# A DLRM tower on one core: the Gram matrices in 128x32 column tiles

## The chip, the cores and the metric

The kernel runs on one NeuronCore of a Trainium2 chip. The metric is the device time of one execution in microseconds (us), the median of three runs. Engines are named as in the profile: PE is TensorE's matmul side and PEld its weight loads, DVE is VectorE, ACT is ScalarE, POOL is GpSimd, SP is SyncE. TensorE's clock has two levels here, 2.4 GHz (a granted clock of 1.0) and 1.2 GHz (0.5).

## The reference, cut to what matters

```python
e = jnp.stack([tbl_0[ids[:, 0]], ..., tbl_26[ids[:, 26]]], axis=1)   # (2048, 27, 128)
dot = jnp.einsum('bnd,bmd->bnm', e, e)                                # one 27x27 Gram per sample
z = dot.reshape(2048, 27 * 27)[:, idx]      # the 351 pairs i < j
h = jnp.concatenate([z, dense_ctx], axis=1)                           # (2048, 367)
h = jnp.maximum(h @ W_top1 + b_top1, 0.0)                             # (2048, 512)
h = jnp.maximum(h @ W_top2 + b_top2, 0.0)                             # (2048, 256)
y = h @ W_top3                                                        # (2048, 1)
```

Everything is float32. Each of 2048 samples takes 27 rows of 128 numbers from 27 tables. Its Gram matrix holds all the dot products of these rows.

## The kernel before, in words

The samples are worked through in 8 bodies (`PAIRS`) of 256 samples, each of 2 tiles (`TILES`) of 128 samples. The first and the last body are written out, and the six between are passes of one loop on every engine (`sweep`). The program is written by hand: each engine has its own list of instructions, and semaphores order them.

Rows come in two ways. For 8 small tables TensorE picks them with one-hot matrices (`lookup`, line 622, four jobs of two tables in a body; VectorE builds the one-hots at line 486). For the other 19 tables GpSimd gathers rows with indirect DMAs (line 331, 38 in a body), and TensorE transposes them (`transpose_rows`, line 639, five jobs per tile). A gather of the next body may start when the transposes of this body have read its rows. In the last body four of the looked-up tables are gathered too (line 338). VectorE and ScalarE take turns to copy both into `embT` (lines 492, 496, 365 and 369), which holds 32 slots of one float for each sample, 27 of them used.

The Gram step (`gram`, line 649) multiplies four samples at once: the stationary operand has the 123 columns of four samples (three slots of 32 and 27 more), the moving one 4 x 26 columns. Only the four diagonal blocks of the product are used. A step has 8 such matmuls, that is 32 samples, and a tile has 4 steps. The steps of a tile use the two tiles `gram_ps[0]` and `gram_ps[1]` in turn. VectorE copies the blocks of the even steps to `blocks` (line 503) and ScalarE those of the odd steps (line 395), with four copies per step, one for each diagonal block (`block_views`). A step may write its bank when the copies of the step two before are done:

```python
past(pe, (gram_dve, gram_act)[s % 2], p * (TILES * STEPS // 2) + step // 2)
```

The transposes use the banks of `gram_ps` too, so that those of the second tile wait for the last copies of the first. When all steps of a tile are copied, VectorE turns the blocks (`turn`, lines 512 to 527) into `z`, and TensorE transposes `z` (line 659) for the three layers (lines 675, 683 and 690; in the last body 707 to 720). These are done one body later, between lookups and transposes. On TensorE a body is in this order:

1. `lookup` 0, transposes of z of the second tile of the body before (`layers` step 0), `lookup` 1, first layer, `lookup` 2 and 3
2. transposes of tile 0, second layer, the four gram steps of tile 0
3. transposes of tile 1, third layer, the four gram steps of tile 1
4. transposes of z of tile 0

In the first body VectorE also builds the first four one-hots of the next body between its block copies: one after each of steps 0 and 2 of each tile. In the other bodies it builds one after step 0 of each tile.

Of the kernel before, what the change touches and what calls it, by code (L numbers as in the profile page):

```python
# [28 lines left out]
ACT = mybir.ActivationFunctionType  # L29

P = 128
B, NF, D, CTX = 2048, 27, 128, 16
# [46 lines left out]
ACT_JOBS = EVERY.all - DVE_JOBS  # L79
NJ = NF - 1  # L80
Q, G = 4, 32
GS = 8
STEPS = G // GS
SHIFTS, RUN = NF // 2, 9
PAIRS_CH = SHIFTS * RUN
# [2 lines left out]
K1 = [PAIRS_CH + n for n in CTX_CH]  # L88
JEXT = NF + SHIFTS
SLOT = 32  # L90
GM = (Q - 1) * SLOT + NF
MLP_JOBS = 6
BANKS = 2
N1, N2 = H1 // P, H2 // P
# [17 lines left out]
def dlrm_tower(nc, ids, ids_mm, ident_in, dense_ctx, tables, W1, b1, W2, b2, W3, out):  # L112
    with ExitStack() as ctx:
        def sb(name, shape, dt):
            return ctx.enter_context(nc.sbuf_tensor(name, shape, dt))

        def ps(name, shape):
            return ctx.enter_context(nc.psum_tensor(name, shape, F32))

        def sem(name):  # L120
            return ctx.enter_context(nc.semaphore(name))

        def sb_view(tile, first, dims, start=0, count=P):
            full = tile[:]
            pitch = full.ap[0][0]
            return bass.AP(full.tensor, start * pitch + first, [[pitch, count], *dims])
# [18 lines left out]
        embT = sb("embT", [P, TILES, P, SLOT], F32)  # L145
        blocks = sb("blocks", [P, TILES, NJ, G], F32)
# [11 lines left out]
        gram_ps = [ps(f"gram_ps{k}", [P, 2, 512]) for k in range(2)]  # L158
# [29 lines left out]
        gram_dve = sem("gram_dve")  # L188
        gram_act = sem("gram_act")
# [7 lines left out]
        def past(eng, s, value):  # L197

            if not (isinstance(value, int) and value <= 0):
                eng.wait_ge(s, value)  # L200
# [28 lines left out]
            return (sb_view(embT, t * P * SLOT + slot, [[1, n], [SLOT, P]]),  # L229
                    emb_bank(jobs, jobs.look + t * jobs.tr + k)[:, 0:n * P].rearrange("d (f b) -> d f b", f=n))  # L230

        def block_views(t, s, q):

            src = gram_ps[s % 2][q * 32:q * 32 + NF, :, 0:4 * Q * NJ].rearrange("i h (g c) -> i h g c", g=4)
            return (sb_view(blocks, t * NJ * G + GS * s, [[4, 2], [1, 4], [G, NJ]], q * 32, NF),
                    src[:, :, :, q * NJ:(q + 1) * NJ])

        block = ctx.enter_context(nc.Block())

# [105 lines left out]
        def _(act):  # L345
# [43 lines left out]
            def keep_blocks(p, t, s):  # L389

                step = t * STEPS + s
                act.wait_ge(gram_filled, p * TILES * STEPS + step + 1)
                past(act, s_turned, (p - 1) * TILES + t + 1)
                for q in range(Q):
                    last = nc.scalar.activation(*block_views(t, s, q), ACT.Copy)  # L395
                last.then_inc(gram_act, 1)

            def last_layers(kind, t):

# [62 lines left out]
        def _(dve):  # L462
# [7 lines left out]
            def convert_ids(p):  # L470
                dve.wait_ge(s_idsb, (p + 1) * 16)

                past(dve, s_onehot, p * NM - len(ACT_ONEHOTS))
                if isinstance(p, int) and p == 1:
                    dve.wait_ge(onehot_act, len(ACT_ONEHOTS))
                nc.vector.tensor_copy(ids_f[:], ids_b[:]).then_inc(s_ids, 1)  # L476
                dve.wait_ge(s_ids, p + 1)

            def make_onehot(p, k):

                if k >= OH:
                    dve.wait_ge(emb_filled, p * EVERY.all + (k - OH) // LOOK_TABLES + 1)
                else:
                    past(dve, emb_filled, (p - 1) * EVERY.all + (k + NM - OH) // LOOK_TABLES + 1)
                for c in range(CH):
                    last = nc.vector.tensor_scalar(onehot[:, k % OH, c, :], ids_f[:, k, :], row_of[:, c:c + 1], None,  # L486
                                                   ALU.is_equal)
                last.then_inc(s_onehot, 1)

            def move_lookup(p, k):  # L490
                dve.wait_ge(emb_filled, p * EVERY.all + k + 1)
                nc.vector.tensor_copy(*lookup_views(k)).then_inc(emb_dve, 1)

            def move_rows(p, jobs, t, k):
                dve.wait_ge(emb_filled, p * EVERY.all + jobs.look + t * jobs.tr + k + 1)
                nc.vector.tensor_copy(*row_views(jobs, t, k)).then_inc(emb_dve, 1)  # L496

            def keep_blocks(p, t, s):

                step = t * STEPS + s  # L500
                dve.wait_ge(gram_filled, p * TILES * STEPS + step + 1)
                for q in range(Q):
                    last = nc.vector.tensor_copy(*block_views(t, s, q))  # L503
                last.then_inc(gram_dve, 1)

            def turn(p, t):

# [48 lines left out]
            def body(p, first, last):  # L556


                jobs = FINAL if last else EVERY
                for k in range(EVERY.look):  # L560
                    if k < jobs.look and jobs.by_dve[k] and not first:
                        move_lookup(p, k)
                    if last:
                        continue
                    if not first and (k + 1) * LOOK_TABLES <= NM - OH:
                        for f in range(k * LOOK_TABLES, (k + 1) * LOOK_TABLES):
                            make_onehot(p, OH + f)
                    if k == 1:
                        convert_ids(p + 1)
                    if k == 2 and not first:  # L570
                        make_onehot(p + 1, 0)
                        make_onehot(p + 1, 1)
                for t in range(TILES):
                    for k in range(jobs.tr):
                        if jobs.by_dve[jobs.look + t * jobs.tr + k]:
                            move_rows(p, jobs, t, k)
                    if t:
                        turn(p, 0)
                    for s in range(0, STEPS, 2):
                        keep_blocks(p, t, s)  # L580
                        if first:
                            make_onehot(p + 1, (t * STEPS + s) // 2)
                        elif not last and s == 0:
                            make_onehot(p + 1, 2 + t)
                turn(p, 1)

            sweep(dve, body)

        @block.tensor
        def _(pe):  # L590
# [51 lines left out]
            def gram(p, t, s):  # L642

                step = t * STEPS + s

                past(pe, (gram_dve, gram_act)[s % 2], p * (TILES * STEPS // 2) + step // 2)
                for g in range(GS):
                    four = embT[:, t, (GS * s + g) * Q:(GS * s + g + 1) * Q, :]
                    last = nc.tensor.matmul(gram_ps[s % 2][0:GM, g // 4, (g % 4) * Q * NJ:(g % 4 + 1) * Q * NJ],  # L649
                                            four.rearrange("d q f -> d (q f)")[:, 0:GM], four[:, :, 0:NJ],  # L650
                                            start=True, stop=True)
                last.then_inc(gram_filled, 1)

            def transpose_z(p, t):
# [125 lines left out]
```

## Time and profile before

| | |
|---|---|
| median of 3 runs | 455.84 us (454.64 to 455.99) |
| the profiled execution | 455.73 us |
| its span, first to last instruction | 453.9 us |
| mean granted TensorE clock | 0.944 |
| TensorE matmuls, weight loads | 372.9 us, 345.7 us busy, 2740 instructions each |
| VectorE, ScalarE, GpSimd | 305.8 us, 183.3 us, 303.8 us busy |
| gram matmuls (line 649) | 1024, 124.6 us busy |
| block copies, ScalarE and VectorE (lines 395, 503) | 128 and 128, 67.8 us and 65.9 us busy |

The span is taken from one profiled execution, and the 1.8 us around it are part of its time. Busy time of TensorE counts each matmul to its modelled end, so that matmuls which follow each other closely overlap in it.

### The profile page before, as it was taken

Reading aid. Unit: us, or ns where it says so; the run is one execution under the profiler, and the core shown is the slowest. Engines: PE = TensorE matmul, PEld = TensorE weight load, DVE = VectorE, ACT = ScalarE, POOL = GpSimd, SP = SyncE. Lnnn points to the kernel's source line nnn. Section 1 sums busy time; section 2 is a strip of 40 time slices with the busy share of each in tenths; the row PEclk is TensorE's granted clock in tenths of the full one; section 3 lists DMA queues with packets and bytes.
Section 4 is the critical chain, followed back from the end, with each engine's and each line's share of the span. In section 5 each row is a group of like instructions: output and inputs, shape, how many; then the busy total and the mean of one; then the engine's idle time right before and its main releaser. Section 6 shows DMA issues by size and latency. Waiting matters only on the chain.

```text
span 453.9 us, 8416 instructions
## 1 busy us (share of the span) xinstructions
PE 372.9 (82%) x2740; PEld 345.7 (76%) x2740; DVE 305.8 (67%) x719; ACT 183.3 (40%) x304; POOL 303.8 (67%) x317
## 2 busy tenths in 40 slices
PE   0652555799998999899988998999989998998577
PEld 0642555698987899689978996989878996997376
DVE  3565505989768886888688968797688867435250
ACT  1117630542444334632455146424443345435152
POOL 5777605777677767777777777777777776777300
PEclk9966865999999999999999999999999999999599
DMA  4645693422125921293225421441269221222100
GB/s 110 179 162 179 173 81 59 131 53 58 38 54 70 133 49 47 60 92 99 53 51 83 111 56 48 79 122 46 53 63 120 69 53 46 55 52 54 29 1 0
DMA packets 28189, 34.85 MB, mean 77 GB/s; under 512 B 12975, under 2 KB 21815, under 8 KB 28174
## 3 DMA queue, kind: packets, MB, share of 16 engines
q1 hardware_dynamic: 18190, 14.19, 20.4%
q0 software_dynamic: 9984, 20.47, 16.7%
q8 instruction: 8, 0.13, 0.1%
q14 instruction: 7, 0.06, 0.0%
HBM read 34.63 MB, written 0.01 MB: 76 GB/s over the span
## 4 chain that ended last, share of the span: by engine, by line
PE 54%; DVE 13%; DMA 12%; ACT 8%; issue 7%; SPq 5%; POOL 1%; POOLq 0%; ACTq 0%; DVEq 0%
PE gram_ps L649 19%; PE emb_ps L622 16%; PE mlp_ps L675 8%; DVE blocks L503 6%; DMA blocks<-in_tbl 6%; PE mlp_ps L683 5%; ACT blocks L395 5%; DMA ids_b<-in_ids_mm 3%; PE gram_ps L639 3%; ACT embT L369 3%; SPq L276 2%; DMA rows<-in_tbl,idx 2%; DVE turned L512 2%; DVE onehot L486 1%; DVE z L527 1%
## 5 line engine op out<-in xcount | busy, mean ns | idle before, releaser
L331 POOL DMA_INDIRECT rows<-in_tbl,idx x304 | 295.9, 973 | 117.5 <-DMA rows<-in_tbl,idx 86.9
L622 PE MATMUL emb_ps<-onehot,parts 125*128 125x256 f32 x960 | 130.2, 297 | 33.9 <-ACT parts L349 20.6
L622 PEld LDWEIGHTS emb_ps<-onehot,parts 125*128 125x128 f32 x960 | 124.6, 202 | 35.8 <-ACT parts L349 21.4
L486 DVE TENSOR_SCALAR onehot<-ids_f,row_of 128x256 fp32r<-128x256 f32 x464 | 143.9, 383 | 9.2 <-PE emb_ps L622 8.6
L649 PE MATMUL gram_ps<-embT 128*123 128x104 f32 x1024 | 124.6, 281 | 23.5 <-DVE embT L496 11.4
L649 PEld LDWEIGHTS gram_ps<-embT 128*123 128x123 f32 x1024 | 119.6, 195 | 31.8 <-DVE embT L496 12.7
L395 ACT ACTIVATE blocks<-gram_ps 27x208 f32<-27x208 f32 x128 | 67.8, 530 | 99.2 <-PE gram_ps L649 98.0
L503 DVE COPY blocks<-gram_ps 27x208 f32<-27x208 f32 x128 | 65.9, 515 | 46.9 <-PE gram_ps L649 45.2
L380 ACT ACTIVATE h<-mlp_ps,b_sb 128x256 f32<-128x256 f32 x42 | 17.6, 471 | 68.1 <-PE mlp_ps L675 53.6
L365 ACT ACTIVATE embT<-emb_ps 128x512 f32<-128x512 f32 x22 | 24.1, 1098 | 46.1 <-PE emb_ps L622 46.1
L496 DVE COPY embT<-gram_ps 128x512 f32<-128x512 f32 x32 | 31.7, 1032 | 13.5 <-PE gram_ps L639 13.4
L639 PE MATMUL gram_ps<-ident,rows 128*128 128x128 f32 x240 | 32.2, 282 | 7.8 <-ACT blocks L395 3.5
L675 PE MATMUL mlp_ps<-zT,w_sb 128*128 128x256 f32 (+1 forms) x168 | 37.5, 378 | 0.0
L639 PEld LDWEIGHTS gram_ps<-ident,rows 128*128 128x128 f32 x240 | 27.1, 144 | 11.5 <-ACT blocks L395 5.5
L675 PEld LDWEIGHTS mlp_ps<-zT,w_sb 128*128 128x128 f32 (+1 forms) x168 | 31.2, 189 | 4.3
L369 ACT ACTIVATE embT<-gram_ps 128x512 f32<-128x512 f32 (+1 forms) x32 | 28.1, 975 | 2.3 <-PE gram_ps L639 2.3
L683 PE MATMUL mlp_ps<-h,w_sb 128*128 128x256 f32 x112 | 25.3, 379 | 0.0
L512 DVE STREAM_TRANSPOSE turned<-blocks 128x832 f32<-128x832 f32 x16 | 16.5, 1028 | 12.8 <-ACT blocks L395 10.7
L683 PEld LDWEIGHTS mlp_ps<-h,w_sb 128*128 128x128 f32 x112 | 20.7, 190 | 2.5
L476 DVE CAST ids_f<-ids_b 128x2048 f32<-128x2048 int32 x7 | 8.6, 1227 | 15.7 <-DMA ids_b<-in_ids_mm 15.5
L369 ACT ACTIVATE embT<-emb_ps 128x512 f32<-128x512 f32 x16 | 17.3, 1080 | 0.2
L659 PE MATMUL mlp_ps<-ident,z 128*128 128x128 f32 x42 | 7.2, 281 | 6.5 <-DVE z L527 6.5
(46 smaller groups left out, 144.6 us busy)
## 6 DMA issues: line engine op xcount, KB each, us to landing
ids_b<-in_ids_mm SPq DMA_DIRECT2D x7, 1024.0 KB
rows<-in_tbl,idx POOLq DMA_INDIRECT x304, 2.5
turned<-in_tbl SPq DMA_DIRECT2D x4, 500.0 KB
h<-in_tbl SPq DMA_DIRECT2D x2, 500.0 KB
blocks<-in_tbl SPq DMA_DIRECT2D x2, 500.0 KB
ids_b<-in_ids_mm SPq DMA_DIRECT2D x1, 768.0 KB
w_sb<-in_W_top SPq DMA_DIRECT2D x1, 512.0 KB
idx<-in_ids SPq DMA_DIRECT2D x16, 13.5 KB, 1.6
```

The lines of the kernel that those rows point to most:

```text
L331: pool.indirect_dma_start(rows[:, t, n, :], None, tables[f], bass.IndirectOffsetOnAxis(idx[:, t, f:f + 1], 0), engine_sem=gathers_written) ...
L369: nc.scalar.activation(*row_views(jobs, t, k), ACT.Copy).then_inc(emb_act, 1)
L395: last = nc.scalar.activation(*block_views(t, s, q), ACT.Copy)
L486: last = nc.vector.tensor_scalar(onehot[:, k % OH, c, :], ids_f[:, k, :], row_of[:, c:c + 1], None, ALU.is_equal)
L496: nc.vector.tensor_copy(*row_views(jobs, t, k)).then_inc(emb_dve, 1)
L503: last = nc.vector.tensor_copy(*block_views(t, s, q))
L512: nc.vector.transpose(turned[:, t, 0:NJ * G], blocks[:, t, :, :].rearrange("p j g -> p (j g)")).then_inc(s_turned, 1)
L622: last = nc.tensor.matmul(emb_ps[k % 2][:, m * W:(m + 1) * W], parts[0:MP, f, part, c * D:(c + 1) * D], onehot[0:MP, f % OH, c, :], start= ...
L639: done = nc.tensor.transpose(emb_bank(jobs, job)[:, m * P:(m + 1) * P], table_rows, ident[:])
L649: last = nc.tensor.matmul(gram_ps[s % 2][0:GM, g // 4, (g % 4) * Q * NJ:(g % 4 + 1) * Q * NJ], four.rearrange("d q f -> d (q f)")[:, 0:GM] ...
L675: last = nc.tensor.matmul(mlp_ps[job % 2][:, m * W:(m + 1) * W], w1_sb[0:K1[c], c, n * P:(n + 1) * P], zT[0:K1[c], c, :], start=(c == 0), ...
L683: last = nc.tensor.matmul(mlp_ps[0][:, m * W:(m + 1) * W], w2_sb[:, n, m * P:(m + 1) * P], h1[:, n, :], start=(n == 0), stop=(n == N1 - 1))
```

## The change

The Gram step now has one matmul per sample. Its stationary operand is the sample's 32 slots (27 rows and 5 zero ones), its moving operand 26 columns, and its output goes to 32 partitions of PSUM: sample q of four goes to partitions 32q to 32q + 31. A step has 64 matmuls, that is 64 samples, and a tile has 2 steps in place of 4. All results of a step lie in one bank, 416 columns wide, and one copy of 128 partitions by 416 columns takes them to `blocks`. VectorE copies step 0 and ScalarE step 1. In the first body VectorE builds two one-hots after its one block copy in each tile. The results in `blocks` lie where they lay before, and 5 more partitions of each 32 are written.

```diff
-GS = 8
+GS = 16
 STEPS = G // GS
-GM = (Q - 1) * SLOT + NF

-        def block_views(t, s, q):
-            src = gram_ps[s % 2][q * 32:q * 32 + NF, :, 0:4 * Q * NJ].rearrange("i h (g c) -> i h g c", g=4)
-            return (sb_view(blocks, t * NJ * G + GS * s, [[4, 2], [1, 4], [G, NJ]], q * 32, NF),
-                    src[:, :, :, q * NJ:(q + 1) * NJ])
+        def block_views(t, s):
+            src = gram_ps[s % 2][:, 0, 0:GS * NJ].rearrange("p (g j) -> p g j", g=GS)
+            return sb_view(blocks, t * NJ * G + GS * s, [[1, GS], [G, NJ]]), src

                 past(act, s_turned, (p - 1) * TILES + t + 1)
-                for q in range(Q):
-                    last = nc.scalar.activation(*block_views(t, s, q), ACT.Copy)
-                last.then_inc(gram_act, 1)
+                nc.scalar.activation(*block_views(t, s), ACT.Copy).then_inc(gram_act, 1)

                 dve.wait_ge(gram_filled, p * TILES * STEPS + step + 1)
-                for q in range(Q):
-                    last = nc.vector.tensor_copy(*block_views(t, s, q))
-                last.then_inc(gram_dve, 1)
+                nc.vector.tensor_copy(*block_views(t, s)).then_inc(gram_dve, 1)

                         keep_blocks(p, t, s)
                         if first:
-                            make_onehot(p + 1, (t * STEPS + s) // 2)
+                            make_onehot(p + 1, 2 * t)
+                            make_onehot(p + 1, 2 * t + 1)
                         elif not last and s == 0:
                             make_onehot(p + 1, 2 + t)

                 for g in range(GS):
-                    four = embT[:, t, (GS * s + g) * Q:(GS * s + g + 1) * Q, :]
-                    last = nc.tensor.matmul(gram_ps[s % 2][0:GM, g // 4, (g % 4) * Q * NJ:(g % 4 + 1) * Q * NJ],
-                                            four.rearrange("d q f -> d (q f)")[:, 0:GM], four[:, :, 0:NJ],
-                                            start=True, stop=True)
+                    for q in range(Q):
+                        one = embT[:, t, (GS * s + g) * Q + q, :]
+                        last = nc.tensor.matmul(gram_ps[s % 2][q * SLOT:(q + 1) * SLOT, 0, g * NJ:(g + 1) * NJ],
+                                                one, one[:, 0:NJ], start=True, stop=True)
                 last.then_inc(gram_filled, 1)
```

## Rows read from the trace of the kernel before

**Rows 1.** The page, parts 1 and 2: busy time; granted clock in 40 slices.
```profile
PE 372.9 (82%) x2740; PEld 345.7 (76%) x2740; DVE 305.8 (67%) x719; ACT 183.3 (40%) x304; POOL 303.8 (67%) x317
...
PEclk9966865999999999999999999999999999999599
```

**Rows 2.** The chain of waits, one steady body: start, us, what.
```profile
232.53 1.09 ACT embT L369 x2
...
245.68 1.05 DVE turned L512
```

**Rows 3.** The timeline of PE in steady bodies: start, us, instructions, idle before.
```profile
222.48 3.58 PE L649 MATMUL gram_ps<-embT 128*123 128x104 f32 x32
226.52 3.84 PE L649 MATMUL gram_ps<-embT 128*123 128x104 f32 x32 [0.46 <-DVE blocks L503]
...
235.29 3.68 PE L649 MATMUL gram_ps<-embT 128*123 128x104 f32 x32 [0.79 <-ACT embT L369]
239.43 3.81 PE L649 MATMUL gram_ps<-embT 128*123 128x104 f32 x32 [0.46 <-DVE blocks L503]
...
248.30 0.54 PE L659 MATMUL mlp_ps<-ident,z 128*128 128x128 f32 x3 [0.95 <-DVE z L527]
...
252.48 5.36 PE L675 MATMUL mlp_ps<-zT,w_sb 128*128 128x256 f32 x24
...
362.29 1.80 PE L639 MATMUL gram_ps<-ident,rows 128*128 128x128 f32 x15
```

**Rows 4.** Groups of instructions, shapes apart: busy us, mean ns, idle before.
```profile
L649 PE MATMUL gram_ps<-embT 128*123 128x104 f32 x1024 | 124.6, 281 | 23.5 <-DVE embT L496 11.4 <-DVE blocks L503 6.5 <-ACT embT L369 4.7
L649 PEld LDWEIGHTS gram_ps<-embT 128*123 128x123 f32 x1024 | 119.6, 195 | 31.8 <-DVE embT L496 12.7 <-DVE blocks L503 8.8 <-issue 7.7
L395 ACT ACTIVATE blocks<-gram_ps 27x208 f32<-27x208 f32 x128 | 67.8, 530 | 99.2 <-PE gram_ps L649 98.0
...
L369 ACT ACTIVATE embT<-gram_ps 128x384 f32<-128x384 f32 x16 | 13.9, 866 | 1.9 <-PE gram_ps L639 1.9
...
L690 PEld LDWEIGHTS mlp_ps<-h,w_sb 128*1 128x1 f32 x28 | 1.8, 85 | 3.5 <-issue 1.9
```

**Rows 5.** The timeline of POOL, three of its 312 gathers.
```profile
121.99 0.94 POOL L331 DMA_INDIRECT rows<-in_tbl,idx  x1 [2.68 <-PE gram_ps L639]
...
365.98 0.94 POOL L331 DMA_INDIRECT rows<-in_tbl,idx  x1 [0.30 <-DMA rows<-in_tbl,idx]
...
423.49 0.94 POOL L338 DMA_INDIRECT late_rows<-in_tbl,idx  x1 [0.30 <-issue]
```

**Rows 6.** The timeline of PE in the last body.
```profile
428.90 4.58 PE L649 MATMUL gram_ps<-embT 128*123 128x104 f32 x32
...
436.07 1.86 PE L649 MATMUL gram_ps<-embT 128*123 128x104 f32 x16
...
444.63 2.84 PE L711 MATMUL mlp_ps<-zT,w_sb 128*128 128x128 f32 x24
```

**Rows 7.** The timeline of PE in the second body.
```profile
103.46 0.54 PE L659 MATMUL mlp_ps<-ident,z 128*128 128x128 f32 x3 [1.08 <-DVE z L527]
...
120.83 1.80 PE L639 MATMUL gram_ps<-ident,rows 128*128 128x128 f32 x15
```

**Rows 8.** Stretches at half clock: length; PE, PEld, DVE, ACT, POOL busy (count); clock; DMA.
```profile
65.60:79.20 13.60, 6.15 (x30) 6.15 (x31) 5.50 (x9) 0.00 (x0) 5.95 (x7) 0.50 0.44 64
...
89.50:92.90 3.40, 3.40 (x19) 3.40 (x18) 1.70 (x4) 0.00 (x0) 2.49 (x4) 0.50 0.29 83
```

**Rows 9.** DMA queues: packets, MB, share of 16 engines.
```profile
q8 instruction: 8, 0.13, 0.1%
```

**Rows 10.** The timeline of DVE, a steady body and the last.
```profile
226.50 2.40 DVE L486 TENSOR_SCALAR onehot<-ids_f,row_of 128x256 fp32r<-128x256 f32 x8
...
440.19 1.04 DVE L512 STREAM_TRANSPOSE turned<-blocks 128x832 f32<-128x832 f32 x1 [2.14 <-issue]
```

**Rows 11.** The timeline of ACT in the last body.
```profile
437.97 2.13 ACT L395 ACTIVATE blocks<-gram_ps 27x208 f32<-27x208 f32 x4 [1.21 <-PE gram_ps L649]
```

## The prediction

> **What bounds the kernel now.** I read the shares first: TensorE is busy 82% of the span, VectorE and GpSimd 67% each, ScalarE 40%, and the granted clock is full from the eighth of 40 slices on but for the end [rows 1]. So the steady state is a TensorE affair, if GpSimd does not stand just behind it. The chain of waits over one steady body says which waits end last: its pieces are TensorE's, with two kinds of break: ScalarE's embT copies after the first gram phase, and the last copies of blocks with VectorE's turning behind them [rows 2]. The PE timeline gives the sizes [rows 3]: a gram phase of one tile runs from 222.48 to 230.19 (226.52 + 3.84, less the 0.28 that one matmul lasts, plus one spacing of 0.11), 7.71 us, the other from 235.29 to 243.07, 7.78 us. Between them lie 5.10 us, the last 0.79 of them a wait for ScalarE's embT copies, and after the second it waits 0.95 us for z. A body repeats every 48.3 us ((362.29 - 120.83)/5 [rows 3, 7]).
>
> GpSimd's gathers are the second chain. One takes 0.94 us with 0.30 us before it; 38 of them make up a body. At 121.99 the engine was idle 2.68 us until TensorE's transposes at 120.83 freed the rows [rows 5, 7]: 2.38 us more than usual. After that it goes at its own pace of 48.8 us a body ((365.98 - 121.99)/5), and by 365.98 it is behind TensorE: the transposes that free those rows began at 362.29, which by the 1.16 us of the first case allows 363.45, so there are 2.5 us of slack [rows 3, 5]. The last gather at 423.49 starts the tail. So a faster TensorE in the steady bodies buys almost nothing by itself: only the 2.38 us and the tail are to be had. A slower one costs in full once 2.5 us are used up.
>
> **The price of a pair.** One fp32 matmul is two LDWEIGHTS/MATMUL pairs (1024 for 512 matmuls [rows 4]). 24 pairs of 256 moving columns take 5.36 us, 24 of 128 take 2.84 us [rows 3, 6]: 105 ns per 128 columns, 0.82 ns a column. The gram's pairs take (3.58 - 0.28)/31 = 106 ns [rows 3, 4], though 104 moving columns make only 85 ns. The load of 123 columns makes 101 and so is the bound, with some 5.5 ns on top. The duration of a load also goes with its columns, 85 ns at 1 column and 195 at 123 [rows 4]. After the change there are 4096 pairs, of 32 weight columns and 26 moving ones: 26.2 + 5.5 = 32 ns by this line, if loads stay hidden behind matmuls and there is no floor. Total 131 us for 109 us. No row shows small pairs. The bounds: below, a next tile's load runs beside the matmul of the one before, 26 x 0.82 = 21 ns, and with four tiles at once some 7 ns; above, nothing in the trace is issued faster than the 106 ns pair. I take 32, the straight line through the rows.
>
> The Trainium skill (TensorEngine Tiling, Instruction Overhead) speaks against the change: each matmul carries about 60 cycles on trn2, so that a free size of 1 costs as much as 60. By that and our 1.2 and 2.4 GHz a pair would cost an estimated 50 or 25 ns; the rows of this trace, all at 104 columns or more, can't tell. The skill (TensorE: Matmul & The Clock Gate, Part 3) speaks for it: matmuls in different column tiles start some 4 ns apart.
>
> **The gram phases.** Two per body, 256 pairs each: 512 x 32 ns = 16.4 us against 15.5, +0.9 us. The waits inside the phases are gone with it, since step 0 now leaves 4.1 us for one copy.
>
> **The copies.** Eight copies of 27x208 per 64 samples, four on each of two engines, 0.53 us one on ScalarE [rows 4], become one of 128x416. ScalarE's strided copy goes from 0.53 at 208 to 0.866 at 384 columns [rows 4], so 0.93 at 416 (from 0.87, the price of 384, to 1.06, twice that of 208). What stands on the path is the last one of a phase, on ScalarE: 4 x 0.53 = 2.12 becomes 0.93, -1.2 us. Between the phases ScalarE's embT copies follow it at 232.53 and end the gap [rows 2, 3], so all of it counts: -1.2. TensorE's transposes no longer wait for the gram banks, but that is inside the same gap. After the second phase z is ready 1.2 us earlier, of which only the wait of 0.95 counts, since the lookup matmuls lie before it: -1.0. VectorE's copy of step 0, taken as dear as ScalarE's, is hidden by step 1's 4.1 us of matmuls; without that cover it would cost its 0.9.
>
> **Switching the array's form**, four times a body: a matmul lasts 0.28 us and its spacing is 0.11 [rows 4], so an emptied array costs at most 0.17 a time, nothing at least. I take 0.1, +0.4 a body. The Trainium skill (TensorEngine Tiling, Key Properties) says that changing the mode drains the engine, which would be the upper end.
>
> **A steady body:** 0.512 x price - 15.5 - 2.2 + 0.4 = -0.9 us at 32 ns. It breaks even at 34 ns.
>
> **The first body** has 9.6 us of its gram phases at half clock, where a pair takes double [rows 7, 8]. At 32 ns the first phase ends 0.6 us later than before. The one-hot builds now come in two pairs behind step 0's copy, 16 instructions of 0.30 us each time (8 take 2.40 [rows 10]); in the second phase (step 0 ends near 94.2, its copy near 95.3) VectorE is thus busy until about 100.1, and z follows its turning by 2.6 us, as from 245.68 to 248.30 [rows 2, 3]: 102.75 where TensorE waited until 103.46 [rows 7]. So z comes 0.7 us earlier, and so do the transposes at 120.83 and the gathers behind them: -0.7 of the possible 2.38. From there GpSimd's own pace carries the shift to the last gather.
>
> **The tail:** from 428.90 the last phase has 256 x 0.032 = 8.2 us, 0.95 for 1.9 us at half clock, 0.33 for z's transposes: last issue 438.4. ScalarE's copy starts 0.3 later, as before (437.97 for a last issue at 436.07 + 1.86 - 0.28), and takes 0.93, so that the turning can start at 439.7, where it did at 440.19 [rows 6, 10, 11]: -0.5.
>
> **Sum:** -0.7 - 0.5 = -1.2 us on the profiled execution's 455.73 (span 453.9 and 1.8 around it): 454.5. The median of the runs is 455.84, 0.1 above that execution; I leave the sum as it is. So eight copies made one and TensorE's steady body 0.9 us shorter disappear almost whole behind the gathers.
>
> **Rivals.**
> *Tiles overlap.* At 21 ns a pair the first body gives the whole 2.38 us, the tail 0.5 + 256 x 0.011 = 3.3: 450.0. Four tiles at once, 7 ns, give 3.6 more: 446. For it: the four samples go to four different column groups. Against: the two halves of an fp32 matmul follow each other in the same group, and load and matmul of one group must alternate. Chance 0.28.
>
> *A fixed cost per pair.* This ends on the other side. The load of one column still lasts 85 ns [rows 4]; if part of that can't be hidden when the matmul before it is itself short, the price is between 32 and 85 + 21. It decides from about 35 ns: each ns more costs 0.5 in the first body, 0.5 in each of five more before the last gathers are released, 0.26 in the tail, 3.3 us in all, after 2.5 us of slack. At 50 ns, the low middle of these: 8.5 + 5 x 8.3 - 2.5 + 4.1 = +52, 507. At 106 ns it would be +240. Chance 0.28, most of it below 50.
>
> *The clock.* The rows at half clock (slices 3 to 7, one near the end) all lie in or behind stretches in which TensorE did little [rows 1, 8]. If the clock falls in the new gram phases as it does there, the gram runs at 1.2 GHz throughout: 64 ns a pair, 11 + 5 x 15.5 - 2.5 + 7 = +93, 549. Against: the gram before kept the full clock, and TensorE is not to idle more than then. Chance 0.08.
>
> *Code.* A body grows from 342 pairs on TensorE (2740 over 8 bodies [rows 1]) to 726. The instruction queue moved 8 packets, 0.13 MB in all, 16 KB each [rows 9], which for six passes of the loop means that the loop's code stayed in the engine. If it no longer fits, each of the five returns waits for at least one block, near 1 us (0.1% of 16 engines' span over 8): TensorE's body loses its 0.9 and the result is 455 to 460. Chance 0.04.
>
> *The straight line, 32 ns*, has 0.32, with its own range 453 to 457: the switches and the load's overhead (5 to 8 ns) move it over both edges of what can be told.
>
> **How the numbers follow.** A measurement of this kernel tells about 0.3%, 1.4 us, from no change. Faster: nearly all of overlap and some of the line, 0.34. Same: 0.23 of the line and the edges of the others, 0.26. Slower: 0.40. For the range, 448 leaves out only four tiles at once; 510 takes in pairs up to 50 ns and leaves out the clock and the dear pairs. Together that leaves out just under 0.2.
>
> **What the profile after would show.** The matmul line of the gram with 4096 entries and the spacing inside a phase: 32 ns is a phase of 8.2 us; under 6 is overlap, over 9 a fixed cost. The granted clock in those phases. One copy of 128x416 near 0.9 us on each engine, 16 each. The gap between the phases near 3.9 us, no wait for z in the steady bodies. Gathers: the first after TensorE's transposes at about 121.3, idle before it 2.0, and the last near 422.8. I am wrong if GpSimd waits for TensorE in every body, if the clock row shows fives, or if TensorE's instruction queue moves some tens of blocks.

## The result, and the profile after

| | before | after |
|---|---|---|
| median | 455.47 us (4 runs) | 449.29 us (4 runs, 448.35 to 449.96) |
| ratio | | 0.9865, 95% interval 0.9839 to 0.9891 |
| profiled execution, span | 455.73, 453.9 us | 449.96, 448.2 us |
| gram matmuls | 1024, 124.6 us busy | 4096, 60.0 us busy |
| block copies, ScalarE and VectorE | 128 and 128, 67.8 and 65.9 us | 16 and 16, 14.7 and 14.2 us |

The change is worth 6.2 us, 1.4%. TensorE lost 49 us of busy time and ScalarE and VectorE 54 us each, and little of that is seen in the end.

The page of the kernel after, parts 1 to 4 (busy time; granted clock; DMA queues; the chain that ended last):

```profile
PE 323.4 (72%) x5812; PEld 286.5 (64%) x5812; DVE 251.4 (56%) x607; ACT 129.5 (29%) x192; POOL 304.4 (68%) x317
...
PEclk9986866589999999999599986998599969957589
...
q8 instruction: 17, 0.28, 0.3%
...
DMA 49%; PE 23%; issue 17%; SPq 5%; POOL 2%; DVE 1%; POOLq 1%; ACT 1%; DVEq 0%
```

In the kernel before, the chain that ended last was this:

```profile
PE 54%; DVE 13%; DMA 12%; ACT 8%; issue 7%; SPq 5%; POOL 1%; POOLq 0%; ACTq 0%; DVEq 0%
```

The chain is now one of gathers: 49% DMA, where it was 12%, and only 23% TensorE. The clock row has fives in the steady bodies, where it was full [rows 1]. The timeline of PE after shows what TensorE does in a steady body:

```profile
205.88 3.85 PE L645 MATMUL gram_ps<-embT 128*32 128x26 f32 x256
209.68 0.63 PE L634 MATMUL emb_ps<-ident,rows 128*128 128x128 f32 x4
210.15 0.60 PE L634 MATMUL gram_ps<-ident,rows 128*128 128x128 f32 x4
213.16 0.63 PE L634 MATMUL gram_ps<-ident,rows 128*128 128x128 f32 x4 [2.40 <-DMA rows<-in_tbl,idx]
218.07 1.09 PE L634 MATMUL gram_ps<-ident,rows 128*128 128x128 f32 x4 [4.28 <-DMA rows<-in_tbl,idx]
221.83 0.87 PE L634 MATMUL gram_ps<-ident,rows 128*128 128x128 f32 x3 [2.68 <-DMA rows<-in_tbl,idx]
```

A gram phase that took 7.71 us [rows 3] takes 3.85, one pair every (3.85 - 0.20)/255 = 14.3 ns, and the time goes into waits for rows, 9.4 us here and 7.6 to 8.5 in the three bodies behind it. The half clock stands in and behind these waits: the granted clock is 1.00 from 205.8 to 209.7, in the gram phase, and 0.50 from 218.0 to 222.7, among the waits.

So the gathers decide when the last body may end, and their last one has not moved. The timeline of POOL after, the first gather of the second body, the first of the third and the last of all:

```profile
70.09 0.94 POOL L329 DMA_INDIRECT rows<-in_tbl,idx  x1 [13.97 <-issue]
...
122.59 0.94 POOL L329 DMA_INDIRECT rows<-in_tbl,idx  x1 [4.79 <-PE gram_ps L634]
...
423.54 0.94 POOL L336 DMA_INDIRECT late_rows<-in_tbl,idx  x1 [0.30 <-issue]
```

The last started at 423.49 before [rows 5] and starts at 423.54 now. From there the end is 30.4 us away before and 24.7 after: between these two executions the whole gain, 5.7 us of span, is in the tail. The timelines of DVE and of PE in the tail after:

```profile
433.91 1.04 DVE L506 STREAM_TRANSPOSE turned<-blocks 128x832 f32<-128x832 f32 x1 [2.63 <-ACT blocks L392]
```

```profile
428.44 1.91 PE L645 MATMUL gram_ps<-embT 128*32 128x26 f32 x125
...
430.84 0.38 PE L645 MATMUL gram_ps<-embT 128*32 128x26 f32 x22
431.79 1.09 PE L645 MATMUL gram_ps<-embT 128*32 128x26 f32 x106 [0.56 <-issue]
```

The turning of the last blocks begins 6.3 us earlier than in [rows 10], and 0.6 of that is lost again in the layers behind it.

TensorE is held back at one place where nothing held it before. The timeline of PE in the first body after:

```profile
71.25 3.16 PE L645 MATMUL gram_ps<-embT 128*32 128x26 f32 x199 [9.09 <-DVE embT L492]
87.50 1.03 PE L645 MATMUL gram_ps<-embT 128*32 128x26 f32 x57 [13.09 <-issue]
```

After 199 of 256 pairs it stands still for 13.09 us, released by nothing that the profile shows. The gathers of the third body, which before waited 2.68 us for TensorE, now wait 4.79, although its work is so much shorter. Of these 2.1 us more, 0.6 come from TensorE, whose transposes begin at 121.43 instead of 120.83. The other 1.5 come from gathers that were done earlier. The gathers of the second body began 1.3 us earlier than in the kernel before (timeline of POOL before):

```profile
71.42 0.94 POOL L331 DMA_INDIRECT rows<-in_tbl,idx  x1 [16.88 <-issue]
```

This early start doesn't come from the Gram step. At 28 us, among the first loads of the program, this execution is already 0.9 us ahead (27.80 against 28.68). Counted from the first gather of the second body, the first one of the third comes 50.6 us later before and 52.5 after.

### The profile page after: what moved, and what is told of

Same layout as the page of the kernel before. It is cut to its first block, busy times and chain, and to the rows that moved or that the text cites. A ratio compares the mean times of both kernels' runs of the same rounds, so it can differ in the third digit from the quotient of the medians.

```text
span 448.2 us, 14298 instructions
## 1 busy us (share of the span) xinstructions
PE 323.4 (72%) x5812; PEld 286.5 (64%) x5812; DVE 251.4 (56%) x607; ACT 129.5 (29%) x192; POOL 304.4 (68%) x317
## 4 chain that ended last, share of the span: by engine, by line
DMA 49%; PE 23%; issue 17%; SPq 5%; POOL 2%; DVE 1%; POOLq 1%; ACT 1%; DVEq 0%
DMA rows<-in_tbl,idx 39%; PE emb_ps L617 7%; DMA blocks<-in_tbl 6%; PE gram_ps L645 5%; DMA ids_b<-in_ids_mm 3%; SPq L274 2%; PE mlp_ps L670 2%; PE gram_ps L634 2%; PE mlp_ps L678 2%; POOL rows L329 1%; PE emb_ps L634 1%; PE mlp_ps L706 1%; DMA late_rows<-in_tbl,idx 1%; SPq L279 1%; POOL late_rows L336 1%
## 5 line engine op out<-in xcount | busy, mean ns | idle before, releaser
L645 PE MATMUL gram_ps<-embT 128*32 128x26 f32 x4096 | 60.0, 202 | 33.4 <-issue 18.6
L645 PEld LDWEIGHTS gram_ps<-embT 128*32 128x32 f32 x4096 | 51.1, 116 | 46.2 <-issue 32.3
L634 PE MATMUL gram_ps<-ident,rows 128*128 128x128 f32 x240 | 39.5, 315 | 45.4 <-DMA rows<-in_tbl,idx 45.4
L634 PEld LDWEIGHTS gram_ps<-ident,rows 128*128 128x128 f32 x240 | 31.8, 163 | 50.4 <-issue 50.3
L498 DVE COPY blocks<-gram_ps 128x416 f32<-128x416 f32 x16 | 14.2, 889 | 53.1 <-PE gram_ps L645 53.0
L367 ACT ACTIVATE embT<-gram_ps 128x512 f32<-128x512 f32 (+1 forms) x32 | 28.7, 950 | 50.6 <-PE gram_ps L634 50.6
L392 ACT ACTIVATE blocks<-gram_ps 128x416 f32<-128x416 f32 x16 | 14.7, 922 | 81.9 <-PE gram_ps L645 81.9
L678 PE MATMUL mlp_ps<-h,w_sb 128*128 128x256 f32 x112 | 27.2, 400 | 0.0
L678 PEld LDWEIGHTS mlp_ps<-h,w_sb 128*128 128x128 f32 x112 | 22.2, 204 | 3.1
L472 DVE CAST ids_f<-ids_b 128x2048 f32<-128x2048 int32 x7 | 9.1, 1304 | 14.9 <-DMA ids_b<-in_ids_mm 14.7
L685 PE MATMUL mlp_ps<-h,w_sb 128*1 128x256 f32 x28 | 11.4, 550 | 0.0
```

Source lines behind the costliest of these rows:

```text
L367: nc.scalar.activation(*row_views(jobs, t, k), ACT.Copy).then_inc(emb_act, 1)
L634: done = nc.tensor.transpose(emb_bank(jobs, job)[:, m * P:(m + 1) * P], table_rows, ident[:])
L645: last = nc.tensor.matmul(gram_ps[s % 2][q * SLOT:(q + 1) * SLOT, 0, g * NJ:(g + 1) * NJ], one, one[:, 0:NJ], start=True, stop=True)
L678: last = nc.tensor.matmul(mlp_ps[0][:, m * W:(m + 1) * W], w2_sb[:, n, m * P:(m + 1) * P], h1[:, n, :], start=(n == 0), stop=(n == N1 - 1))
```

## The experiments

Eight kernels ran, three of them more than once, in five lots on five chips. On two of these chips the kernel before took its usual 455 us. On the other three it took 734 us, and all that ran there is read for single durations and for that chip alone. Ratios are to the kernel before on the same chip, with their 95% intervals.

### Matmuls alone, copies alone

The first kernel has the changed matmuls in the steps and with the copies of before; the second has the matmuls and the 4 steps of before, and one copy of 123x208 per step, which takes the wrong part of the product.

```diff
 # matmuls alone, against the kernel after
-GS = 16
+GS = 8
+            src = gram_ps[s % 2][q * 32:q * 32 + NF, 0, 0:GS * NJ].rearrange("p (g j) -> p g j", g=GS)
+            return sb_view(blocks, t * NJ * G + GS * s, [[1, GS], [G, NJ]], q * 32, NF), src
...
 # copies alone, against the kernel before
+            src = gram_ps[s % 2][0:GM, 0, 0:GS * NJ].rearrange("p (g j) -> p g j", g=GS)
+            return sb_view(blocks, t * NJ * G + GS * s, [[1, GS], [G, NJ]], 0, GM), src
...
-                for q in range(Q):
-                    last = nc.vector.tensor_copy(*block_views(t, s, q))
-                last.then_inc(gram_dve, 1)
+                nc.vector.tensor_copy(*block_views(t, s)).then_inc(gram_dve, 1)
```

They ran first on a chip of 734 us.

> The changed matmuls (one sample per matmul in a 128x32 column tile), but in 4 steps of 32 samples per tile and with four copies of 27x208 per step, as before. My theory: in the tail the matmuls cost some 14.5 ns a pair, 1.9 us a step, but each step must wait for the 2.1 us of copies of the step two before, so that the last phase of the tail ends only about 1 us earlier than before; the gathers end as before. 454 to 455.5 us. Rival, that the matmuls alone bring the gain: 450 us. If the pause in the first body comes back (13 us idle in the gram there), it is not a matter of the step's size.

> The kernel before, its four-sample matmuls untouched, but one copy of 123x208 per step in place of four of 27x208. The copy takes the wrong part of the product, so that everything from z on is computed from other numbers; shapes and amounts of all later work are unchanged. My theory: the last phase of the tail ends 2.2 us earlier (no bank wait, one copy of 0.53 instead of 2.1 at the end), and in the first two bodies TensorE comes up to 2.2 us earlier, which the gathers follow: 451 to 453.5 us. Rival, that copies are hidden and only matmuls count: 455 us.

Measured there: 734.08 us for the matmuls alone (0.9995, 0.9975 to 1.0014) and 704.67 for the copies alone (0.9497, 0.9431 to 0.9562). They ran again on a chip of 454.32 us.

> The same kernel as in the first try of the changed matmuls with the copies of before; there every kernel, the one before too, took 1.6 times its usual time, with TensorE nearly at a stand in its gram phases while gathers ran. What that try did show stands in the numbers here: 8 to 9 ns a pair at full clock. My theory: each step must wait for the 2.1 us of copies of the step two before, so that the tail's last phase ends only 1 us earlier: 454 to 455.5 us. Rival, that the matmuls alone bring the gain: 450 us.

> The kernel before with one copy of 123x208 per step, as in the first try (the copy takes the wrong part of the product; shapes and amounts of all later work are unchanged). My theory: the last phase of the tail ends 2.2 us earlier, and in the first two bodies TensorE comes up to 2.2 us earlier, which the gathers follow: 451 to 453.5 us. Rival, that copies are hidden and only matmuls count: 455 us.

Measured: matmuls alone 455.86 us, 1.0036 (1.0015 to 1.0057), a little slower. Copies alone 450.90 us, 0.9933 (0.9911 to 0.9954). Both lie just outside what was expected, 454 to 455.5 and 451 to 453.5 us. The places follow from three times of each profile, the first gather of the second body, the last gather and the end of the span:

| | second body's first gather | last gather | from the first to the last | span | from the last gather to the end |
|---|---|---|---|---|---|
| before | 71.42 | 423.49 | 352.1 | 453.9 | 30.4 |
| matmuls alone | 70.89 | 426.75 | 355.9 | 454.3 | 27.5 |
| copies alone | 71.47 | 421.17 | 349.7 | 450.5 | 29.3 |
| after | 70.09 | 423.54 | 353.5 | 448.2 | 24.7 |

Each row is one execution, and the starts in the first column spread by 1.4 us. What the gathers lost or gained is therefore better read from the third column than from the second.

The copies alone shorten TensorE's gaps in the first two bodies, and the gathers of the third body no longer wait for it. The timelines of PE and POOL with the copies alone:

```profile
96.62 0.49 PE L654 MATMUL mlp_ps<-ident,z 128*128 128x128 f32 x3
...
113.96 1.80 PE L634 MATMUL gram_ps<-ident,rows 128*128 128x128 f32 x15
```

```profile
118.90 0.94 POOL L330 DMA_INDIRECT rows<-in_tbl,idx  x1 [0.30 <-DMA rows<-in_tbl,idx]
120.15 0.95 POOL L330 DMA_INDIRECT rows<-in_tbl,idx  x1 [0.30 <-DMA rows<-in_tbl,idx]
```

TensorE no longer waits for z (96.62, where it waited until 103.46), the transposes that free the rows come at 113.96 instead of 120.83 [rows 7], and the last gather comes 2.3 us earlier (2.4 counted from the first gather of the second body), which is the 2.38 that the prediction took as the most to be had. The matmuls alone do the reverse. Their pause is there too, and each step waits for the copies of the step two before it. The timelines of PE and POOL with the matmuls alone:

```profile
75.69 1.42 PE L648 MATMUL gram_ps<-embT 128*32 128x26 f32 x71 [1.20 <-DVE blocks L501]
88.27 1.06 PE L648 MATMUL gram_ps<-embT 128*32 128x26 f32 x57 [11.16 <-issue]
...
107.30 0.55 PE L657 MATMUL mlp_ps<-ident,z 128*128 128x128 f32 x3 [1.86 <-DVE z L525]
```

```profile
125.83 0.94 POOL L329 DMA_INDIRECT rows<-in_tbl,idx  x1 [7.70 <-PE gram_ps L637]
```

The gathers of the third body wait 7.70 us, and the last one comes 3.3 us later (3.8 counted from the second body). That eats the 2.9 us that the short matmuls gain in the tail. In the tail the two parts bring 2.9 and 1.1 us alone and 5.7 together: as long as one is missing, the phase still ends with it. I had expected 1 us of the first and 2.2 of the second.

### The same column tile sixteen times in a row

```diff
-                for g in range(GS):
-                    for q in range(Q):
+                for q in range(Q):
+                    for g in range(GS):
```

> The changed kernel with the two loops of a step exchanged: 16 samples in a row go to the same column tile, then 16 to the next. Same instructions, same copies. My theory (loads and matmuls of different column tiles run beside each other, which makes the 14 to 15 ns of a pair): the spacing rises to 21 to 32 ns, a phase from 3.85 us to 5.5 to 8 us, the tail by 1.7 to 4.3 us, the time to 451 to 453.5 us. Rival (a pair of so few columns costs this little whatever its tile): spacing 14 to 15 ns and 449.3 us.

It ran on a chip of 734 us and took 765.12, 1.0412 (1.0381 to 1.0442) of the kernel before there, while its sisters with the tiles in turn took 734 or less. The expected time was for the usual pace and can't be read from this. The price of a pair can be read in the last body, behind the gathers and at full clock. The timelines of PE, first with the tiles in turn (the matmuls alone, same chip), then with this order:

```profile
710.26 1.31 PE L648 MATMUL gram_ps<-embT 128*32 128x26 f32 x128 [0.32 <-DVE embT L494]
```

```profile
740.28 3.93 PE L645 MATMUL gram_ps<-embT 128*32 128x26 f32 x128 [0.32 <-DVE embT L492]
```

128 pairs take (1.31 - 0.20)/127 = 8.7 ns each with the tiles in turn and (3.93 - 0.20)/127 = 29.4 ns in one tile, within the expected 21 to 32. The 8.7 are no matter of that chip: at the usual pace the last 106 pairs of the tail, shown above, take (1.09 - 0.20)/105 = 8.5. The instructions are the same. So it is the neighbouring tiles that work at once, and without that the price is the 32 ns of the straight line through the rows of before, nearly. The Trainium skill (TensorE: Matmul & The Clock Gate, Part 3) says that matmuls of different column tiles start some 4 ns apart, and here the trace agrees in kind, with 8.7 ns for a load and its matmul. The Trainium skill (TensorEngine Tiling, Instruction Overhead) has about 60 cycles for each matmul. There the trace decides: with the tiles in turn there is no such floor, since 8.7 ns are 21 cycles of 2.4 GHz. In one tile 29.4 ns are 71 cycles, and these runs can't tell a floor from the price of the load's columns.

### The ids load held back

The load of ids for the body after next, 1 MB spread over all partitions, starts at 69.46 in the kernel after, just ahead of the pause. Here it waits for the gram of tile 0 of the body before.

```diff
                     sp.wait_ge(s_ids, p + 1)
+                    past(sp, gram_filled, (p - 1) * TILES * STEPS + STEPS)
                     load_ids(p + 1)
```

> The changed kernel; only the 1 MB load of ids for the body after next waits until the gram of tile 0 of the body before is done. My theory: the 13 us pause of TensorE in the first gram phase is the fetch of its next block of code, held up behind this load; without it the pause shrinks under 3 us, the first gathers of the third body no longer wait 4.8 us for TensorE but 0.3, all later gathers come 4.5 us earlier: 444 to 446 us. Rival 1 (the fetch is slow or asked for late in itself): pause of 10 us or more, 449.3 us. Rival 2 (the later load delays the conversion of ids on VectorE in each body): TensorE waits for one-hots, 449 us or more.

> The changed kernel with the later ids load of the first try (1 MB of ids for the body after next, held until tile 0's gram of the body before is done). My theory: the 13 us pause of TensorE in the first gram phase is the fetch of its next block of code, held up behind this load; without it the pause is under 3 us, the first gathers of the third body come about 4.5 us earlier and so do all later ones: 444 to 446 us. Rival 1 (the fetch is slow in itself): pause of 10 us or more, 449.3 us. Rival 2 (the later load delays VectorE's conversion of ids): TensorE waits for one-hots, 449 us or more.

Both ran on chips of 734 us: 705.43 us (0.9596, 0.9558 to 0.9634) and 704.71 us (0.9615, 0.9580 to 0.9650). The third run was on a chip of 454.85 us.

> The changed kernel with the later ids load, once more, since both tries so far fell on a chip where every kernel took 1.6 times its usual time. Read only if the kernel before takes its usual 455 us here. My theory: the 13 us pause of TensorE in the first gram phase is the fetch of its next block of code, held up behind the ids load; without it the pause is under 3 us, the first gathers of the third body come about 4.5 us earlier and so do all later ones: 444 to 446 us. Rival 1 (the fetch is slow in itself, or it is the gathers that hold TensorE up): pause of 10 us or more, 449.3 us. Rival 2 (the later load delays VectorE's conversion of ids): 449 us or more.

Measured: 447.45 us, 0.9840 (0.9805 to 0.9875). The timelines of PE, SP and POOL:

```profile
73.09 3.20 PE L646 MATMUL gram_ps<-embT 128*32 128x26 f32 x199 [8.96 <-DVE embT L493]
77.35 0.84 PE L646 MATMUL gram_ps<-embT 128*32 128x26 f32 x57 [1.06 <-issue]
...
83.11 3.05 PE L646 MATMUL gram_ps<-embT 128*32 128x26 f32 x177 [2.60 <-DVE embT L493]
94.67 1.54 PE L646 MATMUL gram_ps<-embT 128*32 128x26 f32 x79 [8.51 <-issue]
```

```profile
78.69 0.40 SPq L243 DMA_DIRECT2D ids_b<-in_ids_mm  x1
```

```profile
71.49 0.94 POOL L330 DMA_INDIRECT rows<-in_tbl,idx  x1 [16.49 <-issue]
...
120.38 0.94 POOL L330 DMA_INDIRECT rows<-in_tbl,idx  x1 [1.22 <-PE gram_ps L635]
...
421.33 0.94 POOL L337 DMA_INDIRECT late_rows<-in_tbl,idx  x1 [0.30 <-issue]
```

The pause at the 199th pair falls from 13.09 to 1.06 us, though the gathers run beside it as before. A pause of 8.51 us now stands in the second phase, beside the load that starts at 78.69. The instruction queue moves with it. It moves one block in each of these stretches (DMA by stretch, first the kernel after at 72 to 85 us, where no block moves and the ids load does, and at 85 to 87, then this one at 74 to 77 and at 92 to 94):

```profile
q1 hardware_dynamic: 937, 0.94, 47.7%
...
q8 instruction: 1, 0.02, 3.0%
```

```profile
q8 instruction: 1, 0.02, 2.9%
...
q8 instruction: 1, 0.02, 2.9%
```

In the kernel after it moves none between 72 and 85 us, while TensorE stands still from 74.41 on, and here none between 80 and 92. TensorE goes on within some 3 us of the block. The place in the code speaks for this too: the kernel after, this one and the matmuls alone, whose steps are half as long, all stop behind the 199th pair. The first body, the loop's and the last have 3 x 726 pairs for 17 blocks after, and 3 x 342 for 8 before [rows 1, 9], which makes 128 pairs a block both times. From the first stop to the second there are 57 + 19 + 177 = 253 pairs, near two blocks. So the pause is the fetch of the next block of code, and what delays it is the ids load: the pause went where the load went. The gathers of the third body now wait 1.22 us, the last one starts 2.2 us earlier than in the kernel after, and the profiled span falls from 448.2 to 445.9. Counted from the first gather of the second body (71.49 here, 70.09 there) the last one comes 3.6 us earlier. By the medians, taken on different chips, the two ratios to the kernel before still overlap (0.9805 to 0.9875 here, 0.9839 to 0.9891 for the change). The expected 444 to 446 us were missed by 1.5. Of the 4.5 us expected of the last gather, 2.2 came, 0.9 went into the wait that the second pause leaves, and 1.4 were the early start of the kernel after's profiled execution, which this one doesn't have.

### Fewer gathers

To see what the change is worth where gathers don't bind, both kernels ran with 30 gathers in each body after the first. The rows of every fourth table stay those of the first body.

```diff
                         for n in TR[k]:
+                            if n % 4 == 3 and not first:
+                                continue
```

> The changed kernel with 30 instead of 38 gathers in each body after the first (those of every fourth table are left out and the rows of the first body are used again, so that z and all behind it come from other numbers; all other work is unchanged). My theory: in the changed kernel the gathers alone set the 48.8 us of a body, and TensorE's own work is some 39 us, so that a body falls to about 39 us and the time to 385 to 400 us. Rival (TensorE is still near its limit, since its supply of instructions is): 47 us a body, about 440 us.

> The kernel before with the same 30 gathers. My theory: TensorE sets 48.3 us a body there in any case; only its waits for rows in the last body (7 us) go: 446 to 450 us. Together with the run above this prices the change where gathers don't bind: 50 to 60 us. Rival (gathers set the pace in the kernel before too): 48.8 us falls to 45 or less, under 435 us.

They ran on a chip of 733.63 us and took 631.59 (0.8621, 0.8598 to 0.8644) and 663.48 (0.9052, 0.9029 to 0.9075). On that chip the change is worth 32 us of 663 with fewer gathers. But there TensorE is itself held up while gathers run (last section), and my numbers were for the usual pace. They are neither confirmed nor refuted, so the 50 to 60 us stay open.

### A better order

Three moves were put together: the held ids load, the first index loads ahead of the ids and context loads, and VectorE's first conversion of ids behind its first block copy. The second version holds the ids load until both gram phases are done.

```diff
+                if first:
+                    load_next_idx(p)
...
+                    past(sp, gram_filled, (p - 1) * TILES * STEPS + STEPS)   # second version: p * TILES * STEPS
                     load_ids(p + 1)
...
-                    if k == 1:
+                    if k == 1 and not first:
                         convert_ids(p + 1)
...
                         if first:
+                            if t == 0:
+                                convert_ids(p + 1)
```

> The changed kernel with three moves in the order of work: the ids load held as in the first of these runs; in the first body the index loads for the next gathers issued ahead of the ids and context loads; VectorE's conversion of the next ids in the first body after its first block copy. My theory: the gathers of the second body start at about 63.5 us instead of 70 and those of the third no longer wait for TensorE, so that the last gather lands some 11 us earlier: 436 to 440 us. Rival (TensorE's first gram phase, now beside the first ids load, meets the pause for its code again, long enough that the third body's gathers wait): 441 to 446 us.

> The changed kernel with three moves in the order of work: the ids load for the body after next held until both gram phases of the body before are done (so that it meets neither); in the first body the index loads for the next gathers issued ahead of the ids and context loads; VectorE's conversion of the next ids in the first body after its first block copy. Read only if the kernel before takes its usual 455 us. My theory: the first gram phase now starts near 63.5 us and pauses for its code until the first ids load is through (near 72), the second phase has no pause of more than 2 us; the gathers of the second body start near 63.5 us instead of 70 to 71.5, those of the third don't wait for TensorE, the last gather lands near 411.5: 436 to 440 us. Rival (the conversion of ids comes too late in the bodies, or the gathers of the third body still wait): 441 to 448 us.

Both ran on chips of 734 us and took 706.51 (0.9601, 0.9564 to 0.9638) and 705.23 us (0.9595, 0.9575 to 0.9615). That is no more than the held load alone brings there (704.71 and 705.43). Whether the order gives its 10 us at the usual pace stays open.

## Why the prediction was right where it was, and wrong where it was not

**The bound: right.** "A faster TensorE in the steady bodies buys almost nothing by itself: only the 2.38 us and the tail are to be had." The last gather starts at 423.54 against 423.49, and TensorE waits 7.6 to 9.4 us for rows in each of four steady bodies. The gap between the phases, expected near 3.9 us, is therefore 14.1 (209.53 to 223.63): TensorE is now early and waits there. With the copies alone the 2.38 us are taken, 2.3 measured.

**The price of a pair: mis-sized.** I took 32 ns, "if loads stay hidden behind matmuls", and gave the overlap of tiles 0.28. Measured are 14.3 ns over a whole phase, 8.7 ns undisturbed, and 29.4 ns when the tiles don't alternate. The rival was the right one. Its first price of 21 ns, which let only two neighbours overlap, was still too high, and the undisturbed 8.7 is near its second, 7 ns for four tiles at once. This is the term that failed. For a steady body it hardly counts, but the tail's last phase with what came on top had 256 x 32 = 8.2, 0.95 and 0.33 us, 9.5 in all, in the sum, and took 4.3 us from 428.36 to the last issue at 431.79 + 1.09 - 0.20 = 432.68. It also began 0.5 us earlier than the 428.90 that the sum took over.

**The tail: -0.5 predicted, -5.7 measured.** With the measured last issue the sum's own form gives it: the copy starts 0.24 us later and takes 0.90, and the turning starts at 433.91, where 439.7 was predicted. Of these 5.8 us, 0.6 are lost in the layers behind it. The copies' price was right (0.93 predicted, 0.92 on ScalarE over all, 0.89 on VectorE).

**The first body: -0.7 predicted, 0.0 measured.** I had the transposes before the third body's gathers 0.7 us earlier. They came at 121.43 instead of 120.83, because of the 13.09 us pause, which nothing in the sum had. The 0.0 is in part luck. This execution started its second body's gathers 1.3 us early, and counted from there the last gather comes 1.4 us later than before. With the ids load held back it comes 2.2 us earlier, counted in the same way: it was the pause that took this gain. The rival "code" looked at the wrong place. The loop's code stayed in the engine, as I said: the queue moves 17 blocks in all and none between 155 and 375 us. But I asked only whether the loop fits, and not what happens on the way in. So many short pairs run through a block of code (128 pairs, 1.8 us at 14.3 ns) faster than a block can come while 1 MB of ids is on its way. The Trainium skill (Runtime: NRT & Kernel Launch, Instruction fetch mechanics) speaks of blocks of 16 KiB, whose crossing is mostly hidden: the size agrees with this trace (0.28 MB in 17), the hiding does not where a large load lies ahead.

**The clock.** A sign of being wrong was to be "if the clock row shows fives". It does, and the sign was badly chosen: the clock falls where TensorE waits for rows, not because of the form of the matmuls. The prediction's ground, that TensorE would not idle more than before, fell with the price of the pair. In a steady body this time lies within what the gathers allow. In the tail it costs something, since the first pairs of the last phase still run at the lower level (0.50 from 428.4 to 429.4), as the first matmuls there did before (0.55 from 428.9 to 431.0).

**The switches of the array's form** cost little, as predicted: the first transposes start at 209.68, 0.15 us behind the gram's last pair at 205.88 + 3.85 - 0.20. That fits the 0.1 taken and the bound of 0.17, and it is hidden in any case.

**In sum:** the forecast of 454.5 was 5.2 us above the median. On the profiled execution of 449.96 it was 4.5 too high: 5.2 too much in the tail, 0.7 too little ahead of the last gather. The time lay in the range of 448 to 510, but near its lower end, and "slower" had been given the highest chance, 0.40 against 0.34 for faster, while the change was faster by 6 us. That the time comes so near the 450.0 of the overlap rival is luck, because two errors cancelled in it: it had the gathers 2.4 us earlier, and the tail only 3.3 us shorter.

## What to carry to other kernels

When a second chain stands just behind the bound, price the change by what comes after that chain's last link: here 49 us of TensorE's and 108 us of copying engines' time became 6 us, all of it, by the profiles, behind the last gather. A change of instructions and a change of the copies behind them are worth more together than apart (2.9, 1.1 and 5.7 us in the tail), so neither should be judged by its own run. And where instructions become four times as many and much shorter, look at what else is on the DMA queues when their code is first fetched.

## What was unexpected of the hardware

- Pairs of a 128x32 load and a 26-column fp32 matmul come every 8.7 ns when four column tiles take turns, and every 29.4 ns in one tile.
- A block of code took about 1 us to come (the q8 rows: 3.0% of 16 engines over 2 us) but was 13 us late behind a 1 MB broadcast load.
- On three of five chips the kernel before took 734 us, 1.6 times its usual time. In the kernels with the short matmuls TensorE crawled in its gram phases there as long as gathers ran, and recovered 3 to 5 us after the start of the last one ahead of a break. The timelines of PE and POOL, matmuls alone, on such a chip:

```profile
266.45 0.20 PE L648 MATMUL gram_ps<-embT 128*32 128x26 f32 x1 [1.20 <-issue]
268.54 0.20 PE L648 MATMUL gram_ps<-embT 128*32 128x26 f32 x1 [1.89 <-issue]
270.64 0.20 PE L648 MATMUL gram_ps<-embT 128*32 128x26 f32 x1 [1.91 <-issue]
272.73 0.20 PE L648 MATMUL gram_ps<-embT 128*32 128x26 f32 x1 [1.88 <-issue]
...
276.25 1.20 PE L648 MATMUL gram_ps<-embT 128*32 128x26 f32 x70 [0.46 <-issue]
```

```profile
271.99 0.95 POOL L329 DMA_INDIRECT rows<-in_tbl,idx  x1 [0.30 <-issue]
```

  It is not a matter of the short matmuls. With the matmuls of before TensorE stood still there waiting for block copies, and ScalarE, which makes them, waited for what the profile only calls remote. The groups of the kernel before with fewer gathers:

```profile
L655 PE MATMUL gram_ps<-embT 128*123 128x104 f32 x1024 | 157.1, 323 | 180.2 <-ACT blocks L401 113.9 <-DVE blocks L509 30.9 <-issue 28.5
...
L401 ACT ACTIVATE blocks<-gram_ps 27x208 f32<-27x208 f32 x128 | 66.3, 518 | 306.6 <-remote 247.5 <-PE gram_ps L655 58.0
```

  With the copies alone TensorE stood for 17.85 us before 215.12 and ScalarE for 24.59 before 214.55, while gathers ran until 212.30. So more than TensorE is held up while gathers run there; the cause was not found. It is not the ids load: with that held back the kernel took 705 us there, still 1.6 times the 447.45 of the usual pace.
- At the usual pace too a gram phase is not smooth: of its 3.85 us some 1.4 are more than 256 pairs of 8.7 ns need. The weight loads wait 1.0 us in five short stops put down to issue. What makes them was not tried.
